# Graph network kernel: the table fill issued by SP during the counting phase, and all row fetches in the fused rank-and-sum phase

## The chip, the cores and the metric

The kernel runs on one core of a Trainium2 chip. A core has five engines with queues of their own: TensorE (PE: matmuls, and PEld for its weight loads), VectorE (DVE), ScalarE (ACT), GpSimd (POOL) and SyncE (SP), and 16 DMA engines that all of them share. The metric is the device time of one execution in microseconds (us), lower is better.

## The reference, cut to what matters

Four graph layers run one after another over 50,000 nodes of 128 features and 25,000 edges, each followed by a layer norm. The change touches only the first, and of it the part ahead of the matmul:

```python
loops = jnp.arange(N); src = concat([edge_index[0], loops]); dst = concat([edge_index[1], loops])
deg = segment_sum(ones, dst);  dinv = rsqrt(deg)
msg = (x @ W)[src] * (dinv[src] * dinv[dst])[:, None]
h = segment_sum(msg, dst) + b            # then batch norm, relu, x + h
...
x = layernorm(x + L0(x, ...))            # then L1 (routing), L2 (attention), L3 (mean)
```

The kernel sums the rows x[src] times dinv[src] for every dst into a table `agg` in HBM (50,000 x 128, zero where no edge ends), and does the rest from there.

## The kernel before, in words

The program is a row of phases. Each is a Block in which every engine has its own list of instructions; a Block ends when all five engines are through their lists, and a short Block of GpSimd that clears the semaphores follows. Nothing of the next phase starts before that. Edges lie as 200 columns of 128 (T = 200), handled in 50 groups of four columns (EG = 50, GT = 4). The phases that the change touches:

- `ids_phase` (L83): SP loads the src and dst ids with six DMAs (L106 to L109), DVE and PE turn them into columns, SP stores them as rows (L113, L114). ACT issues in this phase, through `fill` (L77), the 49 DMAs that write zeros to all of `agg`, 512 KB each (L80, called at L119).
- `order_phase` (L557): SP loads the dst row once more, shifted by one (L584), PE turns it, and DVE works out which edge is the last of its dst.
- `count_phase` (L207): DVE builds one-hot tiles from the ids in 16 bits (`lows` L254, `highs` L262) and PE adds them up into two histograms (L304); a short chain on DVE, ACT and PE at the end makes the degrees and start positions (L269 to L284). GpSimd fetches the rows x[src] of the first EARLY = 24 groups, one indirect DMA of 128 rows for each column (L242), into the tile `x_src`, which has room for all 200 columns. SP waits for the fill (L233).
- `rank_and_sum_phase` (L325), the fused phase: per column DVE makes one-hot tiles (L428, L431, 16 bit) and compares (L438, L452, L455), PE looks up rank and dinv (L519, L525, L533, L534), ACT weighs the row that was fetched (L504), PE sums edges of one dst (L544, L549), ACT copies the sum to a buffer (L496; US = 3 buffers of a group each). GpSimd fetches the rows of the other 26 groups (L389) and scatters every group's sums to `agg` (L398), four indirect DMAs for each group.
- `moments_phase` reads `agg` and follows.

The order on each queue is written out by `pipeline` (L1549): in step m it calls each stage, in the order given, for the group m minus its lag. For GpSimd it is `pipeline(EG, (late_gather, 0), (scatter, 1))` (L408), where `late_gather` fetches a group in the first two steps and then in every second. A fetch waits only for the fetch four groups before (SC = 4). `scatter(g)` waits until ACT has copied group g; ACT's copy of group g waits for the scatter of group g - 3; ACT's weighing of a column waits for the fetch of its group (L502).

Of the kernel before, what the change touches and what calls it, by code (L numbers as in the profile page):

```python
# [28 lines left out]
SC = 4  # L29
# [3 lines left out]
GT = 4  # L33
EG = T // GT
NJ = 8
NG = N // (P * NJ)
# [46 lines left out]
def ids_phase(k):  # L83

    nc = k.nc
    with ExitStack() as st:
        rows = k.sb(st, "ids_rows_i", [TB, 2, 2, P], I32)
        rows_f = k.sb(st, "ids_rows_f", [TB, 2, 2, P])
        low = k.sb(st, "ids_low_i", [TB, 2, 2, P], I32)
        low_f = k.sb(st, "ids_low_f", [TB, 2, 2, P])  # L90
        cols_i = k.sb(st, "ids_cols_i", [P, 2, T], I32)
        part = k.sb(st, "ids_part_i", [P, 2, 2, T], I32)
        minus = k.sb(st, "ids_minus", [1, 1])
        pt = k.ps(st, "ids_pt", [P, 2, 2, 256])
        padded = k.sem(st, "ids_padded")
        loaded = k.sem(st, "ids_loaded")
        step = k.sem(st, "ids_step")
        turned = k.sem(st, "ids_turned")
        stored = k.sem(st, "ids_stored")
        with nc.Block() as block:  # L100
            @block.sync
            def _(sp):
                sp.wait_ge(padded, 1)
                full = (E // P - TB)
                for a, ids in enumerate((k.src, k.dst)):
                    sp.dma_start(rows[:, a, 0, :], ids[0:TB * P].rearrange("(r e) -> r e", e=P)).then_inc(loaded, 16)  # L106
                    sp.dma_start(rows[0:full, a, 1, :],
                                 ids[TB * P:(TB + full) * P].rearrange("(r e) -> r e", e=P)).then_inc(loaded, 16)
                    sp.dma_start(rows[full:full + 1, a, 1, 0:E - (TB + full) * P],  # L109
                                 ids[(TB + full) * P:E].rearrange("(r e) -> r e", r=1)).then_inc(loaded, 16)  # L110
                sp.wait_ge(step, 3)
                for a, row in enumerate((k.src_row, k.dst_row)):
                    sp.dma_start(row[0:EP].rearrange("(b r e) -> r b e", b=2, e=P), rows_f[:, a]).then_inc(stored, 16)  # L113
                sp.dma_start(k.dst_row[EP:EP + 1].rearrange("(r e) -> r e", r=1), minus[:, :]).then_inc(stored, 16)  # L114
                sp.wait_ge(stored, 48)

            @block.scalar
            def _(act):
                fill(k, act, k.agg, k.zeros[:, :].rearrange("p (j d) -> p j d", j=NJ), k.agg_filled)  # L119

            @block.vector
            def _(dve):
                nc.vector.memset(minus[:, :], -1.0)
                nc.vector.memset(rows[:, :, :, :], PAD_ID).then_inc(padded, 1)
                dve.wait_ge(loaded, 96)
                nc.vector.tensor_copy(rows_f[:, :, :, :], rows[:, :, :, :]).then_inc(step, 1)
                nc.vector.tensor_scalar(low[:, :, :, :], rows[:, :, :, :], 3, 127, ALU.arith_shift_right,
                                        ALU.bitwise_and).then_inc(step, 1)
                dve.wait_ge(step, 2)
                nc.vector.tensor_copy(low_f[:, :, :, :], low[:, :, :, :]).then_inc(step, 1)  # L130

                dve.wait_ge(turned, 1)
                nc.vector.tensor_copy(k.id_col[:, 0, :, :], pt[:, :, 0, 0:T]).then_inc(step, 1)
                nc.vector.tensor_copy(cols_i[:, :, :], pt[:, :, 0, 0:T]).then_inc(step, 1)
                nc.vector.tensor_copy(k.low_col16[:, :, :], pt[:, :, 1, 0:T]).then_inc(step, 1)
                dve.wait_ge(step, 5)
                nc.vector.tensor_scalar(part[:, 0, :, :], cols_i[:, :, :], 10, 3, ALU.arith_shift_right,
                                        ALU.arith_shift_left).then_inc(step, 1)
                nc.vector.tensor_scalar(part[:, 1, :, :], cols_i[:, :, :], 7, None, ALU.bitwise_and).then_inc(step, 1)
                nc.vector.tensor_scalar(k.node_idx[:, :, :], k.id_col[:, 0, :, :], float(N - 1), None, ALU.min)  # L140
                dve.wait_ge(step, 8)
                nc.vector.tensor_tensor(k.high_col[:, :, :], part[:, 0, :, :], part[:, 1, :, :],
                                        ALU.add).then_inc(step, 1)
                dve.wait_ge(step, 9)

            @block.tensor
            def _(pe):
                pe.wait_ge(step, 3)
                for a in range(2):
                    for b in range(2):  # L150
                        nc.tensor.transpose(pt[:, a, 0, b * TB:(b + 1) * TB], rows_f[:, a, b, :], k.ident[0:TB, 0:TB])
                        last = nc.tensor.transpose(pt[:, a, 1, b * TB:(b + 1) * TB], low_f[:, a, b, :],
                                                   k.ident[0:TB, 0:TB])
                last.then_inc(turned, 1)
        k.done = [padded, loaded, step, turned, stored]
        clear_semaphores(nc, k.done)
# [44 lines left out]
        clear_semaphores(nc, [made, step])  # L201


EARLY = 24


def count_phase(k, rows):  # L207


    nc = k.nc  # L210
    with ExitStack() as st:
# [10 lines left out]
        used = k.sem(st, "cnt_used")  # L222
        step = k.sem(st, "cnt_step")
        based = k.sem(st, "cnt_based")
        in0 = list(k.gather_base)
        for u in range(SC):
            k.gather_base[u] += EARLY // SC * 16 * GT
        rooted = k.sem(st, "cnt_rooted")
        with nc.Block() as block:  # L229
            @block.sync  # L230
            def _(sp):

                sp.wait_ge(k.agg_filled, 16 * (NG + 1))  # L233

            @block.gpsimd
            def _(pool):
                for g in range(EARLY + SC):
                    if g >= SC:
                        pool.wait_ge(k.gathered[g % SC], in0[g % SC] + g // SC * 16 * GT)
                    if g < EARLY:  # L240
                        for t in range(g * GT, (g + 1) * GT):
                            nc.gpsimd.indirect_dma_start(  # L242
                                out=rows[:, t, :], out_offset=None, in_=k.x,
                                in_offset=bass.IndirectOffsetOnAxis(ap=k.node_idx[:, 0, t:t + 1], axis=0))\
                                .then_inc(k.gathered[g % SC], 16)

            @block.vector
            def _(dve):
# [44 lines left out]
            def _(pe):  # L293
# [4 lines left out]
                for n in range(T):  # L298
# [4 lines left out]
                    for a in range(2):  # L303
# [4 lines left out]
                pe.wait_ge(step, 4)  # L308
                nc.tensor.matmul(base[:, 0:1], k.before[:, :], scan[:, NCOL - 1:NCOL], start=True,
                                 stop=True).then_inc(based, 1)  # L310
        clear_semaphores(nc, [low_made, hot, used, step, based, rooted, k.agg_filled])


def paced(eng, k, sem, value):
# [10 lines left out]
def rank_and_sum_phase(k, order, rows):  # L325

    nc = k.nc
    with ExitStack() as st:
# [20 lines left out]
                 "ranked", "weighed", "masked", "summed", "copied"]  # L349
        s = {x: k.sem(st, "rank_" + x) for x in names}  # L350
        in0, out0 = list(k.gather_base), list(k.scatter_base)
        for g in range(EARLY, EG):
            k.gather_base[g % SC] += 16 * GT
        for g in range(EG):
            k.scatter_base[g % US] += 16 * GT

        def landed(g):
            return in0[g % SC] + (g - EARLY) // SC * 16 * GT + 16 * GT

        def stored(g):  # L360
            return out0[g % US] + g // US * 16 * GT + 16 * GT
# [1 line left out]
        with nc.Block() as block:  # L363
# [18 lines left out]
            def _(pool):  # L382
                nc.gpsimd.iota(eid[:, :], pattern=[[P, T]], base=0, channel_multiplier=1).then_inc(s["numbered"], 1)

                def gather(g):
                    if g >= EARLY + SC:
                        pool.wait_ge(k.gathered[g % SC], landed(g - SC))
                    for t in range(g * GT, (g + 1) * GT):
                        nc.gpsimd.indirect_dma_start(  # L389
                            out=rows[:, t, :], out_offset=None, in_=k.x,  # L390
                            in_offset=bass.IndirectOffsetOnAxis(ap=k.node_idx[:, 0, t:t + 1], axis=0))\
                            .then_inc(k.gathered[g % SC], 16)
# [7 lines left out]
                            in_=sums[:, g % US, j, :], in_offset=None, bounds_check=N - 1, oob_is_err=False)\  # L400
                            .then_inc(k.scattered[g % US], 16)

                def late_gather(m):
                    g = EARLY + m if m < 2 else EARLY + 1 + m // 2
                    if (m < 2 or m % 2 == 0) and g < EG:
                        gather(g)

                pipeline(EG, (late_gather, 0), (scatter, 1))  # L408
                for g in range(EG - US, EG):
                    pool.wait_ge(k.scattered[g % US], stored(g))  # L410

# [64 lines left out]
            def _(act):  # L476
# [21 lines left out]

                def weigh(n):
                    g = n // GT  # L500
                    if g >= EARLY:
                        act.wait_ge(k.gathered[g % SC], landed(g))  # L502
                    act.wait_ge(s["dinv_picked"], n + 1)
                    nc.scalar.activation(rows[:, n, :], rows[:, n, :], ACT.Copy, scale=k.dinv_src[:, n:n + 1])\  # L504
                        .then_inc(s["weighed"], 1)
# [2414 lines left out]
def build(nc, a, out):  # L2920
# [3 lines left out]
    with ExitStack() as st:  # L2924
        k.paces = k.sem(st, "paces")

        k.agg_filled = k.sem(st, "agg_filled")
        k.gather_base, k.scatter_base = [0] * SC, [0] * (RF + 2)
        k.gathered = [k.sem(st, f"gathered{u}") for u in range(SC)]
        k.scattered = [k.sem(st, f"scattered{u}") for u in range(RF + 2)]  # L2930
# [53 lines left out]
        with ExitStack() as filling:  # L2984
            x_src = k.sb(filling, "x_src", [P, T, D])
            order_phase(k, by_dst, "ord_d")
            count_phase(k, x_src)
            rank_and_sum_phase(k, by_dst, x_src)
        moments_phase(k)
        capsules_phase(k)  # L2990
# [51 lines left out]
```

## Time and profile before

| what | us |
| --- | --- |
| median of 3 runs | 6120.39 (6107.27 to 6133.74) |
| the profiled execution | 6107.41 |
| its span in the trace | 6105.6 |

| stretch of the span, us | phase |
| --- | --- |
| 4.96 to 67.38 | ids phase, with the fill on ACT's queue |
| 68.37 to 80.38 | order phase |
| 81.23 to 336 | count phase with 96 fetches |
| 344.33 to 778 | fused phase with 104 fetches and 200 scatters |
| from 785.34 | moments and all later phases |

Of the later phases two are named: the message phase (3602 to 4156 us) and the mean phase (4970 to 5517), in which GpSimd fetches and scatters all 200 columns (`segment_sum_phase`, L642, L707 and L719), four and four for each group. Times in a row are from the start of the span. In a timeline row the columns are start, duration, engine, line, operation, output and inputs, count, and in brackets the idle time of the engine just before and what ended it. "issue" there means that the engine waited for nothing that the profile shows.

### The profile page before, as it was taken

To read this page: it belongs to the slowest core of one execution; us is meant where nothing else is said; L and a number is where in the kernel's file an instruction comes from. 1 tells how busy PE (TensorE), PEld (TensorE's weight loads), DVE (VectorE), ACT (ScalarE), POOL (GpSimd) and SP (SyncE) were. 2 spreads that over 40 slices of the span, in tenths; PEclk is the share of its full clock that TensorE was granted. 3 is DMA by queue.
4 is the path that set the end of the run, shared out by engine and by line. 5 is a ranking of instruction groups with operands and counts; after the bars stand their busy time and mean duration, and the time that the engine had idled before them with its cause. 6 is when DMAs were issued, how large, how long until landed. Compare 5 with 4: busy or idle time off the path is not lost. (4 is left out here: it accounts for less than half of the span.)

```text
span 6105.6 us, 71185 instructions
## 1 busy us (share of the span) xinstructions
PE 3580.9 (59%) x20428; PEld 2837.0 (46%) x20428; DVE 3790.8 (62%) x11171; ACT 2487.7 (41%) x5939; POOL 2997.5 (49%) x2581
## 2 busy tenths in 40 slices
PE   3379955874111366630667337666999956664443
PEld 0046644773000255530666225554777745554442
DVE  5579944996222466522777656664766635556998
ACT  0046554994000255520222114443666631124666
POOL 4867702730777433376777127772111137772221
PEclk9789977997555689855888655667999977776666
DMA  4023387883444577621555647773434436665554
GB/s 178 24 82 107 99 322 254 254 253 121 130 147 151 189 254 251 204 83 43 154 155 155 214 105 264 262 260 119 147 140 138 142 102 210 211 217 175 188 187 147
DMA packets 555804, 1043.94 MB, mean 171 GB/s; under 512 B 102981, under 2 KB 320489, under 8 KB 549102
## 3 DMA queue, kind: packets, MB, share of 16 engines
q1 hardware_dynamic: 447424, 830.52, 41.0%
q0 software_dynamic: 92800, 157.14, 8.9%
q10 hardware_dynamic: 15192, 51.73, 2.2%
q8 instruction: 167, 2.74, 0.2%
q14 instruction: 221, 1.81, 0.1%
HBM read 663.92 MB, written 387.58 MB: 172 GB/s over the span
## 5 line engine op out<-in xcount | busy, mean ns | idle before, releaser
L1911 PE MATMUL ro_end<-vals,end_mask 128*2 128x128 f32 x1600 | 243.9, 318 | 569.2 <-DVE vals L1775 472.1
L2078 POOL DMA_INDIRECT sc_rows<-layer,node_idx x400 | 388.3, 971 | 155.9 <-issue 121.5
L1911 PEld LDWEIGHTS ro_end<-vals,end_mask 128*2 128x2 f32 x1600 | 148.4, 96 | 655.4 <-DVE vals L1775 483.7
L2524 POOL TENSOR_TENSOR tf_rest<-tf_rest,tf_msum 128x1024 f32<-128x1024 f32 (+1 forms) x49 | 128.8, 2628 | 627.8 <-DMA tf_rest<-rest 627.8
L2587 ACT ACTIVATE tf_hidden<-tf_h_ps,tf_b 128x512 f32<-128x512 f32 x392 | 268.8, 687 | 233.0 <-PE tf_h_ps L2626 222.5
L2638 PE MATMUL tf_o_ps<-tf_w,tf_hidden 128*128 128x128 f32 (+1 forms) x3136 | 358.0, 275 | 0.0
L1937 PE MATMUL ro_acc<-vals,ro_mask 128*126 128x128 f32 x1600 | 246.3, 319 | 187.6 <-ACT ro_square L1869 140.7
L1713 POOL DMA_INDIRECT ro_far<-layer,w_far x200 | 214.7, 1074 | 287.7 <-DVE ro_y L1752 227.1
L2638 PEld LDWEIGHTS tf_o_ps<-tf_w,tf_hidden 128*128 128x128 f32 (+1 forms) x3136 | 353.9, 192 | 0.5 <-issue 0.5
L1235 POOL DMA_INDIRECT sorted<-payload,rank x200 | 198.2, 991 | 316.3 <-POOLq L70 252.0
L2626 PE MATMUL tf_h_ps<-tf_x_t,tf_w 128*128 128x512 f32 x784 | 349.9, 599 | 5.1 <-ACT tf_hidden L2587 3.9
L707 POOL DMA_INDIRECT msg_rows<-values,s_eid x200 | 211.1, 1055 | 272.4 <-POOLq L70 211.8
L937 PE MATMUL ml_conv_out<-op_w_t,ml_conv_tsb 128*128 128x128 f32 (+1 forms) x784 | 177.2, 418 | 281.3 <-DVEq L2864 277.7
L2840 POOL TENSOR_TENSOR ml_scaled<-ml_scaled,op_gamma 128x1024 f32<-128x1024 f32 (+1 forms) x49 | 116.2, 2371 | 450.0 <-ACT ml_scaled L1020 450.0
L1937 PEld LDWEIGHTS ro_acc<-vals,ro_mask 128*126 128x126 f32 x1600 | 227.6, 228 | 210.4 <-issue 175.2
L1726 POOL TENSOR_TENSOR vals<-ro_both,ro_weight 126x1024 f32<-126x1024 f32 x75 | 144.9, 1933 | 336.3 <-ACT ro_weight L1893 333.9
L937 PEld LDWEIGHTS ml_conv_out<-op_w_t,ml_conv_tsb 128*128 128x128 f32 (+1 forms) x784 | 165.3, 320 | 293.9 <-ACT ml_conv_tsb L923 286.4
L242 POOL DMA_INDIRECT x_src<-in_x_dram,node_idx x96 | 222.7, 2320 | 109.4 <-SPq L229 80.5
L1759 DVE TENSOR_TENSOR ro_both<-ro_far,ro_y 128x1024 f32<-128x1024 f32 x25 | 31.0, 1238 | 392.1 <-DMA ro_y<-layer,w_own 392.1
L707 POOL DMA_INDIRECT mean_rows<-x,node_idx x200 | 215.0, 1075 | 118.3 <-POOLq L70 57.7
L1739 POOL DMA_INDIRECT layer<-ro_far,w_last x200 | 215.3, 1076 | 96.5 <-issue 60.4
L398 POOL DMA_INDIRECT agg<-rank_sums,d_last x200 | 212.0, 1060 | 74.4 <-issue 60.9
(474 smaller groups left out, 11932.6 us busy)
## 6 DMA issues: line engine op xcount, KB each, us to landing
ro_mask<-masks SPq DMA_DIRECT2D x100, 504.0 KB, 4.9
si_both<-layer SPq DMA_DIRECT2D x48, 1024.0 KB, 6.1
ro_far<-far SPq DMA_DIRECT2D x75, 512.0 KB, 6.1
ro_both<-both SPq DMA_DIRECT2D x75, 512.0 KB, 6.1
agg<-zeros ACTq DMA_DIRECT2D x48, 512.0 KB
mom_x<-in_x_dram SPq DMA_DIRECT2D x48, 512.0 KB, 9.2
mom_agg<-agg SPq DMA_DIRECT2D x48, 512.0 KB, 7.7
y<-mom_y SPq DMA_DIRECT2D x48, 512.0 KB, 8.5
```

The lines of the kernel that those rows point to most:

```text
L242: nc.gpsimd.indirect_dma_start(out=rows[:, t, :], out_offset=None, in_=k.x, in_offset=bass.IndirectOffsetOnAxis(ap=k.node_idx[:, 0, t:t + ...
L398: nc.gpsimd.indirect_dma_start(out=k.agg, out_offset=bass.IndirectOffsetOnAxis(ap=order.last_idx[:, t:t + 1], axis=0), in_=sums[:, g % US, ...
L707: nc.gpsimd.indirect_dma_start(out=rows[:, g % SS, j, :], out_offset=None, in_=table, in_offset=bass.IndirectOffsetOnAxis(ap=index[:, t:t ...
L937: mm = self.k.nc.tensor.matmul(self.out[b][0:p, j, :], self.turned_sb[:, 4 * b + j, 0:p], self.weight, start=plain, stop=plain or j == 3, ...
L1713: nc.gpsimd.indirect_dma_start(out=rows, out_offset=None, in_=k.layer1_halves, in_offset=bass.IndirectOffsetOnAxis(ap=column[real, t:t + 1 ...
L1739: nc.gpsimd.indirect_dma_start(out=k.layer1_halves, out_offset=bass.IndirectOffsetOnAxis(ap=wide.last[real, t:t + 1], axis=0), in_=sent[re ...
L1911: mm = nc.tensor.matmul(end_ps[0:2, j, :], k.end_mask[:, t, :], k.vals[:, t, :], start=True, stop=True, skip_group_check=True)
L1937: mm = nc.tensor.matmul(acc[w][real, j, :], mask[:, u, j, :], k.vals[:, tile(n, j), :], start=True, stop=True, skip_group_check=True)
L2078: nc.gpsimd.indirect_dma_start(out=rows[:, g % SC, c * GT + j, :], out_offset=None, in_=k.layer1, in_offset=bass.IndirectOffsetOnAxis(ap=k ...
L2587: nc.scalar.activation(hidden[:, h, b, :], h_ps[b][:, :], ACT.Relu, bias=b1[:, b:b + 1]).then_inc(s["bent"], 1)
L2626: nc.tensor.matmul(h_ps[b][:, :], w1[:, b * P:(b + 1) * P], x_t[:, u, 4 * h:4 * h + 4, :].rearrange("p j e -> p (j e)"), start=True, stop= ...
L2638: mm = nc.tensor.matmul(o_ps[h][0:p, j, :], hidden[:, h, b, j * P:j * P + p], w2[:, b, :], start=b == 0, stop=b == NB - 1)
```

## The change

ACT's fill in the ids phase goes away; SP issues the same 49 DMAs at the start of the count phase and waits for them there. GpSimd does nothing in the count phase. In the fused phase it fetches all 50 groups, one in each step, and scatters with a lag of three groups and not one.

```diff
@@ ids_phase
-            @block.scalar
-            def _(act):
-                fill(k, act, k.agg, k.zeros[:, :].rearrange("p (j d) -> p j d", j=NJ), k.agg_filled)
@@ count_phase
-        in0 = list(k.gather_base)
-        for u in range(SC):
-            k.gather_base[u] += EARLY // SC * 16 * GT
+        filled = k.sem(st, "cnt_filled")
...
             def _(sp):
-                sp.wait_ge(k.agg_filled, 16 * (NG + 1))
-            @block.gpsimd
-            def _(pool):
-                for g in range(EARLY + SC):
-                    if g >= SC:
-                        pool.wait_ge(k.gathered[g % SC], in0[g % SC] + g // SC * 16 * GT)
-                    if g < EARLY:
-                        for t in range(g * GT, (g + 1) * GT):
-                            nc.gpsimd.indirect_dma_start(
...
+                fill(k, sp, k.agg, k.zeros[:, :].rearrange("p (j d) -> p j d", j=NJ), filled)
+                sp.wait_ge(filled, 16 * (NG + 1))
@@ rank_and_sum_phase
-            return in0[g % SC] + (g - EARLY) // SC * 16 * GT + 16 * GT
+            return in0[g % SC] + g // SC * 16 * GT + 16 * GT
...
-                    if g >= EARLY + SC:
+                    if g >= SC:
                         pool.wait_ge(k.gathered[g % SC], landed(g - SC))
...
-                def late_gather(m):
-                    g = EARLY + m if m < 2 else EARLY + 1 + m // 2
-                    if (m < 2 or m % 2 == 0) and g < EG:
-                        gather(g)
-                pipeline(EG, (late_gather, 0), (scatter, 1))
+                pipeline(EG, (gather, 0), (scatter, 3))
...
-                    if g >= EARLY:
+                    if n % GT == 0:
                         act.wait_ge(k.gathered[g % SC], landed(g))
```

GpSimd's queue before, from the clearing ahead of the count phase (L74) into the fused phase; `x_src` are fetches and `agg` scatters:

```order
L74 ISA x5
L70 UNCONDITIONAL_BRANCH
L235 UNCONDITIONAL_BRANCH
L242 DMA x_src<-in_x_dram,node_idx 128x128 x96
L229 UNCONDITIONAL_BRANCH
L71 UNCONDITIONAL_BRANCH
L74 ISA x7
L70 UNCONDITIONAL_BRANCH
L381 UNCONDITIONAL_BRANCH
L383 IOTA rank_eid 128x200
L389 DMA x_src<-in_x_dram,node_idx 128x128 x8
L398 DMA agg<-rank_sums,d_last 50000x128 x4
```

The same queue of the changed kernel, with the first groups of the fused phase:

```order
L74 ISA x7
L70 UNCONDITIONAL_BRANCH
L361 UNCONDITIONAL_BRANCH
L363 IOTA rank_eid 128x200
L369 DMA x_src<-in_x_dram,node_idx 128x128 x16
L378 DMA agg<-rank_sums,d_last 50000x128 x4
L369 DMA x_src<-in_x_dram,node_idx 128x128 x4
L378 DMA agg<-rank_sums,d_last 50000x128 x4
```

The 96 fetches ahead of the phase are gone, the phase starts with 16 fetches and not with 8, and then fetches and scatters alternate by fours (before: 4 fetches, 8 scatters). SP's queue before, from the end of the ids phase to the fused phase:

```order
L114 DMA dst_row<-ids_minus 1x1
L100 UNCONDITIONAL_BRANCH
L573 UNCONDITIONAL_BRANCH
L584 DMA ord_d_next<-dst_row 100x2x128
L572 UNCONDITIONAL_BRANCH
L230 UNCONDITIONAL_BRANCH
L229 UNCONDITIONAL_BRANCH
L364 UNCONDITIONAL_BRANCH
L369 DMA rank_src_b<-src_row 128x512
```

SP's queue of the changed kernel at the same place:

```order
L114 DMA dst_row<-ids_minus 1x1
L100 UNCONDITIONAL_BRANCH
L548 UNCONDITIONAL_BRANCH
L559 DMA ord_d_next<-dst_row 100x2x128
L547 UNCONDITIONAL_BRANCH
L221 UNCONDITIONAL_BRANCH
L80 DMA agg<-zeros 128x1024 x48
L80 DMA agg<-zeros 106x1024
L220 UNCONDITIONAL_BRANCH
L344 UNCONDITIONAL_BRANCH
L349 DMA rank_src_b<-src_row 128x512
```

The 49 DMAs of the fill now stand behind the ids and the shifted row, and ahead of nothing but the end of the count phase.

## Rows read from the trace of the kernel before

**Rows 1.** Busy time by engine in stretches of the first 480 us.
```profile
core 0: us, PE busy (x) PEld busy (x) DVE busy (x) ACT busy (x) POOL busy (x), PEclk, DMA share, GB/s
0.00:67.00 67.00, 1.60 (x8) 1.29 (x8) 7.63 (x26) 0.00 (x0) 0.92 (x7) 1.00 0.93 368
...
130.00:180.00 50.00, 29.81 (x133) 7.69 (x132) 50.00 (x164) 0.00 (x0) 50.00 (x1) 1.00 0.00 0
...
244.00:344.00 100.00, 0.00 (x0) 0.00 (x0) 0.00 (x0) 0.00 (x0) 67.91 (x72) 0.50 0.17 48
...
380.00:480.00 100.00, 100.00 (x492) 66.27 (x491) 99.13 (x434) 60.29 (x198) 77.64 (x74) 1.00 0.36 98
```
**Rows 2.** Timeline of the ids and order phases.
```profile
4.96 62.42 ACTq L80 DMA_DIRECT2D agg<-zeros  x49
...
5.68 0.42 SPq L106 DMA_DIRECT2D ids_rows_i<-in_src_dram  x1
...
9.63 1.18 SPq L109 DMA_DIRECT2D ids_rows_i<-in_dst_dram  x1
...
15.14 0.43 DVE L126 CAST ids_rows_f<-ids_rows_i 100x512 f32<-100x512 int32 x1 [9.49 <-DMA ids_rows_i<-in_dst_dram]
...
20.34 0.57 DVE L142 TENSOR_TENSOR high_col<-ids_part_i 128x400 f32<-128x400 int32 x1
...
68.37 0.28 SPq L584 DMA_DIRECT2D ord_d_next<-dst_row  x1
...
77.86 0.59 PE L634 MATMUL ord_d_pt<-ident,ord_d_next 100*128 100x100 f32 x2 [59.84 <-DMA ord_d_next<-dst_row]
...
80.11 0.27 DVE L619 CAST d_last<-ord_d_cols 128x200 int32<-128x200 f32 x1
...
81.26 1.29 DVE L254 TENSOR_TENSOR cnt_hot_low<-iota_row,low_col 128x512 f16<-128x512 f16 x2 [0.88 <-PEq L70]
```
**Rows 3.** Timeline of the second order phase, with no fill beside it.
```profile
1487.63 0.28 SPq L584 DMA_DIRECT2D ord_s_next<-sorted_row  x1
...
1489.85 0.60 PE L634 MATMUL ord_s_pt<-ident,ord_s_next 100*128 100x100 f32 x2 [2.87 <-DMA ord_s_next<-sorted_row]
```
**Rows 4.** Timeline of the count phase and of the next start.
```profile
88.74 1.93 DVE L262 TENSOR_SCALAR cnt_hot_high<-iota_high,high_col 128x392 f16<-128x392 f16 x8
...
91.79 1.93 DVE L262 TENSOR_SCALAR cnt_hot_high<-iota_high,high_col 128x392 f16<-128x392 f16 x8
...
92.48 1.81 PE L304 MATMUL cnt_table<-cnt_hot_high,cnt_hot_low 128*128 128x392 f16 x8 [1.25 <-DVE cnt_hot_high L262]
...
124.69 2.75 POOL L242 DMA_INDIRECT x_src<-in_x_dram,node_idx  x1 [0.30 <-issue]
127.75 107.32 POOL L242 DMA_INDIRECT x_src<-in_x_dram,node_idx  x1 [0.31 <-issue]
...
229.27 1.92 DVE L262 TENSOR_SCALAR cnt_hot_high<-iota_high,high_col 128x392 f16<-128x392 f16 x8
...
232.32 1.92 DVE L262 TENSOR_SCALAR cnt_hot_high<-iota_high,high_col 128x392 f16<-128x392 f16 x8
...
235.37 0.94 POOL L242 DMA_INDIRECT x_src<-in_x_dram,node_idx  x1 [0.30 <-issue]
...
332.79 0.94 POOL L242 DMA_INDIRECT x_src<-in_x_dram,node_idx  x1 [0.30 <-issue]
...
242.48 0.43 DVE L284 TENSOR_SCALAR start<-cnt_scan,cnt_base 128x392 f32<-128x392 f32 x1
...
344.36 0.29 POOL L383 IOTA rank_eid<- 128x200 int32 x1 [10.62 <-POOLq L70]
```
**Rows 5.** Groups of instructions on GpSimd in the first 900 us.
```profile
L398 POOL DMA_INDIRECT agg<-rank_sums,d_last x200 | 212.0, 1060 | 74.4 <-issue 60.9 <-ACT rank_sums L496 13.4
...
L389 POOL DMA_INDIRECT x_src<-in_x_dram,node_idx x104 | 112.4, 1080 | 31.8 <-issue 31.8
```
**Rows 6.** Timeline of GpSimd in the fused phase.
```profile
368.64 1.51 POOL L398 DMA_INDIRECT agg<-rank_sums,d_last  x1 [13.14 <-ACT rank_sums L496]
...
488.48 0.99 POOL L389 DMA_INDIRECT x_src<-in_x_dram,node_idx  x1 [0.30 <-issue]
...
504.79 0.99 POOL L389 DMA_INDIRECT x_src<-in_x_dram,node_idx  x1 [0.30 <-issue]
...
753.29 0.98 POOL L398 DMA_INDIRECT agg<-rank_sums,d_last  x1 [0.30 <-issue]
...
774.20 0.98 POOL L398 DMA_INDIRECT agg<-rank_sums,d_last  x1 [0.30 <-issue]
```
**Rows 7.** Busy time of GpSimd's fetches (L707, 200 each) in two later phases.
```profile
4970.00:5517.00 547.00, 215.02 (x200) 0.77 0.63 204
3602.00:4156.00 554.00, 211.08 (x200) 0.61 0.75 252
```
**Rows 8.** Busy time by engine in stretches of the mean phase.
```profile
5050.00:5250.00 200.00, 138.91 (x749) 119.56 (x750) 110.79 (x129) 41.13 (x112) 155.13 (x148) 0.78 0.64 208
...
5205.00:5210.00 5.00, 0.77 (x4) 0.50 (x4) 3.43 (x4) 0.00 (x0) 4.03 (x4) 0.84 0.67 245
5210.00:5215.00 5.00, 5.00 (x20) 4.24 (x20) 2.62 (x4) 1.11 (x4) 3.84 (x4) 0.50 0.16 49
```

More of the change, by code:

```diff
@@ L201, in constants_phase, with count_phase @@
         clear_semaphores(nc, [made, step])
-EARLY = 24
-def count_phase(k, rows):
+def count_phase(k):
     nc = k.nc
@@ L231, in _ @@
             def _(sp):
-                sp.wait_ge(k.agg_filled, 16 * (NG + 1))
-            @block.gpsimd
-            def _(pool):
-                for g in range(EARLY + SC):
-                    if g >= SC:
-                        pool.wait_ge(k.gathered[g % SC], in0[g % SC] + g // SC * 16 * GT)
-                    if g < EARLY:
-                        for t in range(g * GT, (g + 1) * GT):
-                            nc.gpsimd.indirect_dma_start(
-                                out=rows[:, t, :], out_offset=None, in_=k.x,
-                                in_offset=bass.IndirectOffsetOnAxis(ap=k.node_idx[:, 0, t:t + 1], axis=0))\
-                                .then_inc(k.gathered[g % SC], 16)
+                fill(k, sp, k.agg, k.zeros[:, :].rearrange("p (j d) -> p j d", j=NJ), filled)
+                sp.wait_ge(filled, 16 * (NG + 1))
             @block.vector
@@ L310, in _ @@
                                  stop=True).then_inc(based, 1)
-        clear_semaphores(nc, [low_made, hot, used, step, based, rooted, k.agg_filled])
+        clear_semaphores(nc, [low_made, hot, used, step, based, rooted, filled])
 def paced(eng, k, sem, value):
@@ L351, in rank_and_sum_phase @@
         in0, out0 = list(k.gather_base), list(k.scatter_base)
-        for g in range(EARLY, EG):
+        for g in range(EG):
             k.gather_base[g % SC] += 16 * GT
@@ L2925, in build @@
         k.paces = k.sem(st, "paces")
-        k.agg_filled = k.sem(st, "agg_filled")
         k.gather_base, k.scatter_base = [0] * SC, [0] * (RF + 2)
@@ L2986, in build @@
             order_phase(k, by_dst, "ord_d")
-            count_phase(k, x_src)
+            count_phase(k)
             rank_and_sum_phase(k, by_dst, x_src)
```

## The prediction, made before the changed kernel had run

> **What bounds the kernel now.** I read the stretches of busy time first, to see which phases have an engine that is never idle, and then the timeline of each phase that the change touches.
>
> The count phase is in two halves [rows 1]. From 130 to 180 DVE is busy all of the time and so is GpSimd, but GpSimd with one instruction. From 244 to 344 nothing works but GpSimd. The timeline says why [rows 4]: while DVE makes its 16-bit one-hots, a fetch takes 2.75 us and then one takes 107.32 us; as soon as DVE is through, at 235, it takes 0.94 us plus 0.30 of issue. So only 17 of the 96 fetches were given out beside the counting, and the other 79 run from 235.37 to 333.73 with no cover. DVE's chain had ended at 242.91, and the fused phase begins at 344.36.
>
> The ids and order phases wait for the fill [rows 1, 2]: the DMA engines are 93% busy with it, ACT is busy issuing it until 67.38 though the ids were ready at 20.91, and the shifted row, issued at 68.37, lands only before 77.86 because it stands behind the rest of the fill.
>
> The fused phase is bound twice over. PE and DVE are busy for 100% and 99% of 380 to 480 [rows 1]. GpSimd shows 77.6% there, which looks like room, but every indirect DMA has 0.30 us of "issue" before it, and from the first scatter on the two group rows hold no other idle time to speak of (60.9 and 31.8 us of "issue" in 198 and 104 gaps, 13.4 of waiting, nearly all of it the one wait before the first scatter) [rows 5, 6]. A block of 4 fetches and 8 scatters takes 504.79 - 488.48 = 16.31 us and serves two groups, just what DVE and PE need: 8.15 us a group. In the mean phase, where GpSimd issues 8 indirect DMAs a group, it is busy for 155.13 us of 200, 78% as well [rows 8]. That share is therefore GpSimd's full speed.
>
> **Part 1, the fill leaves the ids phase.** The order phase and the count phase start earlier. Counting from before's own rows [rows 2]: the six loads start at 5.68; the last is issued at 9.63 and the data are there at 15.14. Without 25 MB in the queues I take the issue at 8 and the landing 3 us later, 11. The landing is an estimate between the 2.2 us of the small load with free queues [rows 3] and the 5.5 us here. DVE's and PE's chain from there takes 20.91 - 15.14 = 5.8, to 16.8, with SP's stores beside it. The end of the Block takes 68.37 - 67.38 = 1.0. The shifted row takes 2.2 and not 9.5 [rows 3]. From there to the first one-hot 81.26 - 77.86 = 3.4. Counting starts at 23.4 and not at 81.26: **-58 us**. Bounds: if the ids land no sooner than before, -53; if all small transfers are faster by another 2 us, -60.
>
> **Part 2, the fill in the count phase.** SP has nothing else there. 49 issues took 62.4 us and the rest drained in some 10 more, so it is over at about 96 and DVE's counting, 161.65 us long, at 185. I cost it at nothing; the cover is 89 us thick. Nothing is queued behind SP's wait but the end of the phase. The loads of the fused phase come after it, as they came after SP's wait before. No row shows DVE counting beside such a transfer; a slowing by 1% of the 73 us that it lasts would be under 1 us.
>
> **Part 3, no fetches in the count phase.** The phase ends after DVE's chain, 161.65 us from its start. The Block end costs 81.26 - 80.38 = 0.9 where GpSimd has issued no DMA [rows 2]; behind 96 fetches it cost 10.6 [rows 4]. The fused phase starts 0.9 us behind DVE's chain and not 344.36 - 242.91 = 101.4: **-100 us**. Upper bound of the time: with the 10.6 kept, -91. DVE's speed does not change: a group of four columns took 91.79 - 88.74 = 3.05 us beside the fetches and 232.32 - 229.27 = 3.05 when GpSimd gave out nothing [rows 4].
>
> **Part 4, 96 more fetches on GpSimd's queue in the fused phase.** This is a cost, since that queue has no free time. Before, from its start at 344.36 to the end of the last scatter at 775.18 it is 430.8 us. Now: 16 fetches at 1.25 plus 0.7, 20.7 us. The first scatter waits until ACT has copied group 0, as before 24.3 us behind the start, so 13 us of idle time shrink to 3.5. Then 384 indirect DMAs without a gap.
>
> Their price, with the 0.30 in it: before, 296 of them took 775.18 - 368.64 = 406.5, that is 1.373 each. Undisturbed ones take 0.98 + 0.30 (scatter) and 0.94 + 0.30 (fetch) [rows 4, 6], 376 us for the 296; so 30 us are delays. If the delays stay as many as DVE's 16-bit instructions, the 384 cost 486 + 30 = 516. If they grow with the number of DMAs, 525. In the mean phase 400 of them took 547 in all, 1.367 with waits [rows 7]. I take 1.35 x 384 = 518. With 24.3 ahead it is 542.7: **+112 us**. Bounds: no delays at all, 486, +80; the price of the slower later phase, 554 / 400 = 1.385 [rows 7], +125.
>
> Whether a group now waits on something else: DVE and PE need 8.15 us a group and GpSimd gives one every 10.8, so they wait for the fetch (ACT's wait ahead of weighing) some 2.6 us each group. The scatter of group g stands behind the fetch of g + 3, when group g was copied long ago, so GpSimd waits for nobody. The tail stays: the last scatter, then 10 us to the moments phase.
>
> The Trainium skill (SBUF — State Buffer, section "Who interferes with whom") says that a DVE instruction in a two-port mode and GpSimd lock each other out for a whole instruction, first come first served. By that rule the delays follow the number of DVE's instructions, which is the 516 above and not the 525; both lie within 5 us of what I took.
>
> **Sum.** -58 - 100 + 112 = -46. On the profiled execution 6107.4 - 46 = 6061.4; on the median, which is 13 us above it, 6120.4 - 46 = **6074.4 us**, a ratio of 0.9925. Unknowns at their ends: -60 - 101 + 80 = -81, 6039; -53 - 91 + 125 = -19, 6101.
>
> **Rivals.**
>
> *PE's clock falls a little in the new pauses.* Now PE never rests in the fused phase and the granted clock is 1.00. In the mean phase a stretch in which PE did 0.77 us of work in 5 is followed by one at 0.50, that is 1.2 GHz, though PE is then busy throughout [rows 8]; over that phase it is 0.77, and 0.61 over the other [rows 7]. For it: the new pauses of 2.6 us come once a group. Against it: in counting PE pauses 1.25 us in every 3.05 and keeps 1.00 [rows 1, 4]; and the effect checks itself, since a slower PE fills its own pause. Price: at the mean phase's 0.77 a group takes PE 8.15 / 0.77 = 10.6 us, still inside GpSimd's 10.8. At 0.73 it is 11.2, 50 x (11.2 - 8.15) = 152 on the phase: -6 in all, 6114. No difference, chance 0.10.
>
> *The clock falls for good, and the kernel is slower.* The same mechanism in force: at the message phase's 0.61 [rows 7] a group takes 8.15 / 0.61 = 13.4 us, 50 x 5.25 = 262 us on the phase: +104, 6224. It decides from 8.15 + 158 / 50 = 11.3 us a group on, a mean clock of 0.72. Chance 0.06. The Trainium skill (TensorE: Matmul & The Clock Gate, section "HAM oscillation") warns of this: a kernel that waits for a transfer in each round restarts cold in each round. The row of 5210 agrees that it happens; no row shows it for pauses of 2.6 us after 8 us of unbroken work.
>
> *GpSimd's indirect DMAs get cheaper.* With DVE idle a quarter of the time, its locks fall into gaps: the lower bound of part 4, +80, 6042. Chance 0.08.
>
> *The moved work is not hidden at all or not moved.* The queue listings show it moved, so I give it nothing.
>
> **How the numbers follow.** Forecast with its bounds 0.76, of which 0.07 lie at the upper edge within 0.5%. A measurement of this kernel can tell about 0.5% (31 us) from no change. Faster by more: 0.69 + 0.08 = 0.77. Within: 0.07 + 0.10 = 0.17. Slower: 0.06. The range takes the bounds 6039 and 6101 with a few us of scatter between runs: 6040 to 6104. It leaves out the two clock cases and slips at the edges, 0.2.
>
> **What the changed profile would show.** Part 1: first one-hot of counting at 22 to 28. Part 3: the fused phase begins 162.5 us behind it, near 186. Part 2: the fill's DMAs on SP's queue from there, landed before 105, and DVE's groups still 3.05 us. Part 4: GpSimd without gaps above 0.3 us from the first scatter, 10.6 to 11 us from group to group, PE busy 75 to 80%, and ACT's largest wait the one for `x_src`. Wrong it would be if DVE is still at 99% there (then GpSimd had room), if the granted clock in the fused phase is below 0.9, or if the last scatter comes earlier than 515 or later than 560 us behind the start.

## The result, and the profile after

| | before | changed |
| --- | --- | --- |
| median, us | 6121.7 (4 runs, 6107.3 to 6133.7) | 6071.7 (4 runs, 6060.0 to 6076.7) |
| span of the profiled execution, us | 6105.6 | 6074.9 |
| ratio | | 0.9917, 95% interval 0.9889 to 0.9944 |

The changed kernel is 50 us faster by the medians. The forecast was 6074.4 with a range of 6040 to 6104.

The ids and order phases of the changed kernel, timeline (the answer to [rows 2]):

```profile
7.48 0.28 SPq L109 DMA_DIRECT2D ids_rows_i<-in_dst_dram  x1
9.32 0.43 DVE L122 CAST ids_rows_f<-ids_rows_i 100x512 f32<-100x512 int32 x1 [3.67 <-DMA ids_rows_i<-in_dst_dram]
...
14.51 0.56 DVE L138 TENSOR_TENSOR high_col<-ids_part_i 128x400 f32<-128x400 int32 x1
...
16.12 0.28 SPq L559 DMA_DIRECT2D ord_d_next<-dst_row  x1
...
18.18 0.59 PE L609 MATMUL ord_d_pt<-ident,ord_d_next 100*128 100x100 f32 x2 [5.99 <-DMA ord_d_next<-dst_row]
...
21.58 1.29 DVE L234 TENSOR_TENSOR cnt_hot_low<-iota_row,low_col 128x512 f16<-128x512 f16 x2 [0.88 <-PEq L70]
```

The ids land at 9.3 and not at 15.1, the shifted row 2.1 us after its issue and not 9.5, and counting starts at 21.58 and not at 81.26. The largest piece lies between the two: the ids are ready at 15.07 and the order phase begins 1.05 us later, where before it began 47.46 us after the ids were ready (20.91 to 68.37), since the Block could not end while ACT was still issuing. Of the 59.7 us, 46.4 are this wait for ACT's issuing, 5.8 the landing of the ids and 7.4 the shifted row. The busy times by stretch (the answer to [rows 1]):

```profile
core 0: us, PE busy (x) PEld busy (x) DVE busy (x) ACT busy (x) POOL busy (x), PEclk, DMA share, GB/s
0.00:20.00 20.00, 2.19 (x10) 1.58 (x10) 8.77 (x31) 0.00 (x0) 0.92 (x7) 1.00 0.09 25
20.00:80.00 60.00, 36.91 (x156) 10.58 (x156) 59.05 (x194) 1.28 (x1) 0.00 (x0) 1.00 0.98 389
80.00:180.00 100.00, 56.60 (x252) 14.82 (x250) 99.75 (x316) 0.53 (x1) 0.00 (x0) 0.99 0.06 23
...
400.00:500.00 100.00, 84.60 (x369) 54.29 (x370) 74.42 (x319) 44.97 (x151) 76.81 (x77) 0.93 0.35 91
```

From 20 to 80 the DMA engines are 98% busy with the fill, and DVE counts beside them; the fill is over long before the counting. The row of before in which only GpSimd worked has gone. In the fused phase, in the stretch from 400 to 500, DVE has fallen from 99% to 74%, PE from 100% to 85%, and GpSimd stands at 77%, as before. Its rows (the answer to [rows 4] and [rows 6]):

```profile
182.66 0.43 DVE L264 TENSOR_SCALAR start<-cnt_scan,cnt_base 128x392 f32<-128x392 f32 x1
184.27 0.29 POOL L363 IOTA rank_eid<- 128x200 int32 x1 [182.71 <-POOLq L70]
```

```profile
440.76 0.99 POOL L369 DMA_INDIRECT x_src<-in_x_dram,node_idx  x1 [0.31 <-issue]
...
451.12 1.00 POOL L369 DMA_INDIRECT x_src<-in_x_dram,node_idx  x1 [0.30 <-issue]
...
462.16 0.99 POOL L369 DMA_INDIRECT x_src<-in_x_dram,node_idx  x1 [0.31 <-issue]
...
721.45 0.98 POOL L378 DMA_INDIRECT agg<-rank_sums,d_last  x1 [0.30 <-issue]
```

One group takes 10.4 and 11.0 us, and the gaps are 0.3 us of issue. The groups of GpSimd, and who waited for whom in the phase (engine, line, waited for: us in total, times, longest):

```profile
L378 POOL DMA_INDIRECT agg<-rank_sums,d_last x200 | 207.3, 1037 | 63.4 <-issue 60.4 <-ACT rank_sums L471 3.0
L369 POOL DMA_INDIRECT x_src<-in_x_dram,node_idx x200 | 205.9, 1029 | 61.2 <-issue 60.3 <-ACT rank_sums L471 0.9
```

```profile
ACT rank_low_hot L463 <- PE rank_turned L494: 117.1, 148, 2.5
DVE rank_picked L427 <- PE rank_look L509: 99.3, 68, 5.9
ACT rank_sums L471 <- DMA agg<-rank_sums,d_last: 82.5, 30, 5.1
...
ACT x_src L479 <- DMA x_src<-in_x_dram,node_idx: 47.8, 26, 4.2
```

GpSimd waited for work once, 2.74 us ahead of the first scatter at 208.87; the rest of the 3.0 and 0.9 us put down to ACT are gaps of 0.30 us like all others. ACT waits for GpSimd through its scatters and its fetches. Its longest wait in total, the 117.1 us for PE, is no sign of that: it was there before (114.4).

All kernels of this study run the same instructions from the moments phase on. This table takes the main points of each profiled execution apart, from their timelines and groups (us; "chain" is from the first one-hot to the start of the last instruction of DVE's chain, "fused" from the start of the phase to the start of the last scatter, "rest" from the first load of the moments phase to the end of the span):

| kernel | counting starts | chain | fused starts | fused | moments start | rest |
| --- | --- | --- | --- | --- | --- | --- |
| before | 81.3 | 161.2 | 344.4 | 429.8 | 785.3 | 5320.3 |
| changed | 21.6 | 161.1 | 184.3 | 537.2 | 729.7 | 5345.3 |
| e1_fill_only | 21.9 | 161.2 | 287.6 | 429.7 | 728.4 | 5327.2 |
| e2_fetch_only | 80.9 | 161.1 | 243.6 | 538.0 | 789.8 | 5341.4 |
| e3_early_4_groups | 21.8 | 161.2 | 185.0 | 516.0 | 708.9 | 5329.9 |
| e4_early_12_groups | 21.9 | 161.3 | 226.3 | 477.0 | 715.4 | 5338.0 |
| e5_lag_2 | 21.9 | 161.1 | 184.6 | 541.6 | 734.1 | 5334.8 |
| e7_two_input_onehots | 22.5 | 283.9 | 308.0 | 476.9 | 797.0 | 5341.5 |
| e8_paced_dve | 22.1 | 162.4 | 195.9 | 476.1 | 684.2 | 5340.6 |
| e9_paced_tighter | 26.3 | 163.6 | 191.6 | 476.7 | 680.4 | 5331.1 |
| e10_early_24_paced | 26.7 | 163.1 | 247.6 | 430.7 | 689.4 | 5328.8 |
| e11_early_24_one_wait | 26.4 | 161.3 | 274.9 | 431.0 | 717.0 | 5343.3 |

The rest varies by 25 us from one execution to the next, with no order in it. That is the scatter of this measurement, and the reason why the two profiled spans differ by 31 us and the medians by 50. Where two kernels have the same instructions in the first 730 us, the pieces agree within about 1 us (537.2 and 538.0; 477.0, 476.9, 476.1 and 476.7), so these can be compared closely, the whole only by the median of several runs.

### The profile page after: what moved, and what is told of

Read it like the earlier page. It is cut to its first block and busy times, and to the rows that moved or that the text cites. A ratio compares the mean times of both kernels' runs of the same rounds, so it can differ in the third digit from the quotient of the medians.

```text
span 6074.9 us, 71017 instructions
## 1 busy us (share of the span) xinstructions
PE 3601.1 (59%) x20317; PEld 2864.6 (47%) x20428; DVE 3792.9 (62%) x11171; ACT 2480.6 (41%) x5939; POOL 2876.7 (47%) x2581
## 3 DMA queue, kind: packets, MB, share of 16 engines
q8 instruction: 167, 2.74, 0.2%
## 5 line engine op out<-in xcount | busy, mean ns | idle before, releaser
L1714 POOL DMA_INDIRECT layer<-ro_far,w_last x200 | 221.0, 1105 | 96.1 <-issue 60.3
L694 POOL DMA_INDIRECT msum<-msg_sent,s_last x200 | 206.4, 1032 | 77.6 <-issue 59.2
L694 POOL DMA_INDIRECT agg<-mean_sums,d_last x200 | 210.8, 1054 | 62.9 <-issue 60.3
```

Of the source, the lines that this page charges most:

```text
L694: nc.gpsimd.indirect_dma_start(out=dest, out_offset=bass.IndirectOffsetOnAxis(ap=order.last_idx[:, t:t + 1], axis=0), in_=sent[:, g % SS, ...
L1714: nc.gpsimd.indirect_dma_start(out=k.layer1_halves, out_offset=bass.IndirectOffsetOnAxis(ap=wide.last[real, t:t + 1], axis=0), in_=sent[re ...
```

## The experiments

**Which part brings the gain.** Two kernels, each with one part of the change. The first:

```diff
 # before.py, count_phase; ACT's fill in the ids phase removed
             def _(sp):
+                fill(k, sp, k.agg, k.zeros[:, :].rearrange("p (j d) -> p j d", j=NJ), k.agg_filled)
                 sp.wait_ge(k.agg_filled, 16 * (NG + 1))
```

> The kernel before with the fill alone moved: SP issues it at the start of the count phase; the 96 fetches beside the counting stay. Theory (fill is the whole net gain, the move of the fetches is neutral: 100 us saved in the count phase, 107 added in the fused phase, 3 back at its end): counting starts near 21.6 us in the span and not at 81.3, the fused phase starts near 284.7, and all of -60 us stays: ratio to before 0.990 (6062 against 6122), within 0.3% of the changed kernel. Rival (the fill's move alone gives little since GpSimd's fetches bound the count phase and the fill slows them): -20 us or less, ratio 0.997 or more.

Measured: 6057.5 us, ratio 0.9899 (0.9884 to 0.9913). The second, the fetches alone:

```diff
 # changed kernel, ids_phase
+            @block.scalar
+            def _(act):
+                fill(k, act, k.agg, k.zeros[:, :].rearrange("p (j d) -> p j d", j=NJ), k.agg_filled)
 # count_phase
-                fill(k, sp, k.agg, k.zeros[:, :].rearrange("p (j d) -> p j d", j=NJ), filled)
-                sp.wait_ge(filled, 16 * (NG + 1))
+                sp.wait_ge(k.agg_filled, 16 * (NG + 1))
...
```

> The changed kernel with the fill put back on ACT's queue in the ids phase; all 200 fetches in the fused phase. Theory: count phase 100 us shorter, fused phase 107 us longer, end of it 3 us shorter, so ratio to before 1.000 to 1.001 (+4 us). Rival (moving the fetches is where the gain is, as the 100 us without other work in the count phase suggest): -40 us, ratio 0.993.

Measured: 6125.1 us, ratio 1.0006 (0.9995 to 1.0017). The table shows the pieces: fetches in the fused phase start it 100.4 us earlier behind the counting (162.7 and not 263.1 us after the first one-hot), make it 108 us longer, and save 3 us at its end (7.2 and not 10.2 us from the end of the last scatter to the moments phase). The whole gain of the change is the fill's 60 us. The first kernel, without the move, is even a little faster by its median (6057.5 against 6071.7), though the intervals of the two ratios overlap; up to the moments phase they lie 1.3 us apart. Moving the fetches has no effect that the medians can tell from none (up to the moments phase it costs 4.5 us), since GpSimd's time was only carried from a place where it stood alone to one where it stands alone again.

**Is it GpSimd's stream that bounds the fused phase?** If so, each indirect DMA taken out of the phase is worth 1.34 us there. Sixteen of them go beside the counting:

```diff
 # changed kernel, count_phase
+            @block.gpsimd
+            def _(pool):
+                for g in range(EARLY):                    # EARLY = 4
+                    for t in range(g * GT, (g + 1) * GT):
+                        nc.gpsimd.indirect_dma_start(out=rows[:, t, :], ...)
...
 # rank_and_sum_phase, fetches spread evenly between the scatters
-                pipeline(EG, (gather, 0), (scatter, 3))
+                fetched = EARLY
+                for g in range(EG):
+                    while fetched < min(EG, EARLY + 4 + -(-g * (EG - EARLY - 4) // (EG - 4))):
+                        gather(fetched)
+                        fetched += 1
+                    scatter(g)
```

> The changed kernel with the first 4 groups (16 fetches) issued beside the counting, without a wait between them; the other 184 spread evenly over the fused phase. Theory (GpSimd's instruction stream is the bound of the fused phase at 1.34 us for each indirect DMA): 16 x 1.34 = 21 us less in the fused phase, 517 and not 538, the count phase as long as in the changed kernel, so ratio to before 0.988 (6050). Rival (ACT's waits for scatters, 82 us in the changed kernel, bound it rather than the number of DMAs): the fused phase stays at 535 or more.

Measured: 6041.3 us, ratio 0.9878 (0.9859 to 0.9896). The phase took 516.0 us where 517 was expected. With 12 groups out early it took 477.0 where 474 was expected (e4, below). That is 1.2 to 1.3 us for each DMA taken out. With 24 groups it took 430.7 (e10, below), the floor, where PE and DVE are at 100 and 99% again.

The other candidate was the wait of ACT for a buffer, of which the prediction had said nothing:

```diff
-                pipeline(EG, (gather, 0), (scatter, 3))
+                pipeline(EG, (gather, 0), (scatter, 2))
```

> The changed kernel with the scatters two groups and not three behind the fetches. In the changed kernel ACT waits 82.5 us for a buffer that a scatter still holds, and 47.8 for fetched rows; the prediction had named only the latter. Theory (GpSimd's stream of 400 indirect DMAs at 1.34 us is the bound, the waits of the others are its shadow): the phase stays at 537 +- 4 us, ACT's wait only shifts from scatters to fetches, ratio to the changed kernel 1.000 +- 0.002. Rival (the wait for buffers costs time by itself): the phase falls by 10 us or more.

Measured: 6070.7 us, ratio to before 0.9912 (0.9897 to 0.9927), the changed kernel 0.9917. The fused phase took 541.6 us, 4.5 more, just past the expected 537 +- 4.

```profile
ACT x_src L479 <- DMA x_src<-in_x_dram,node_idx: 122.1, 47, 3.8
```

ACT's wait for scatters is gone from the longest waits and the one for fetches has grown from 47.8 to 122.1, with nothing gained. These waits are the shadow of one queue; which of them is seen depends on the order in it. The 4.5 us are GpSimd's own, and all lie in one place: only 12 fetches and not 16 stand ahead of the first scatter now, so it waits there 7.19 us for ACT's first copy and not 2.74. After that every gap is 0.30 us again.

**Why were the fetches beside the counting held?** In [rows 4] the 17th fetch takes 107 us. It is also the first with a semaphore wait ahead of it. Twelve groups without any wait between them:

> As the one with 4 groups, but 12 groups (48 fetches) beside the counting, with no semaphore wait between the groups (before had one ahead of the 17th fetch, the one that took 107 us). Theory A (the wait ahead of the fifth group is what held GpSimd until DVE ended): all 48 go at 3.05 us each, over by 170 us, hidden; the fused phase falls to 24 + 336 x 1.34 = 474; ratio to before 0.981 (6007). Theory B (whatever the waits, GpSimd gets no more than some 16 fetches out while DVE makes 16-bit one-hots): the 17th again takes over 100 us, the other 31 follow at 1.25 behind DVE's end, the fused phase starts 40 us later; ratio 0.988 (6048).

Measured: 6055.3 us, ratio 0.9892 (0.9878 to 0.9906). Theory B, and with less than 16. Timeline of GpSimd with 4 groups early, where there are only 16 fetches and no wait:

```profile
56.06 2.75 POOL L237 DMA_INDIRECT x_src<-in_x_dram,node_idx  x1 [0.30 <-issue]
59.12 116.49 POOL L237 DMA_INDIRECT x_src<-in_x_dram,node_idx  x1 [0.30 <-issue]
175.91 0.94 POOL L237 DMA_INDIRECT x_src<-in_x_dram,node_idx  x1 [0.30 <-issue]
```

It was the 14th here, the 13th with 12 groups, the 15th in e1 and the 17th in before. Neither the semaphore nor a count of 16 decides it: the fetch is let go when DVE's counting ends. Where the slow ones end is seen in the fourth fetch of before, beside DVE's row of 88.74 to 90.67 in [rows 4]:

```profile
88.04 2.75 POOL L242 DMA_INDIRECT x_src<-in_x_dram,node_idx  x1 [0.30 <-issue]
```

It ends 0.1 us behind the last of the eight TENSOR_SCALARs, and so do the others of 2.75 us. The long ones end 0.7 to 0.8 us behind the last TENSOR_SCALAR ahead of the end of DVE's counting (234.25 and 235.07 in before). This points at the TENSOR_SCALARs, the only instructions with one 16-bit input in DVE's loop. The next kernel is the one with 12 groups with another form of them:

```diff
-                        nc.vector.tensor_scalar(hot_high[:, n % 4, a, :], k.iota_high16[:, :],
-                                                k.high_col[:, a, n:n + 1], None, ALU.is_equal).then_inc(hot, 1)
+                        nc.vector.scalar_tensor_tensor(hot_high[:, n % 4, a, :], k.iota_high16[:, :],
+                                                       k.high_col[:, a, n:n + 1], ones16[:, :], ALU.is_equal,
+                                                       ALU.mult).then_inc(hot, 1)
```

> The one with 12 groups beside the counting, with the one-hots of the high ids made by an instruction with two inputs from SBUF (compare, then times a tile of ones) and not with one: same output, other form on DVE, which costs DVE more, up to 96 us in all. Theory (it is DVE's 16-bit one-input form that shuts GpSimd out): no fetch takes more than 3 us, most near 1, and all 48 are out within 70 us of the start of counting. Rival (any DVE work without gaps does it): again one fetch of over 100 us.

Measured: 6140.3 us, a single run and so without an interval; the instruction takes 622 ns and not 304, so counting took 284 us, more than I had allowed for. And the theory fell, as did its rival:

```profile
52.39 5.20 POOL L238 DMA_INDIRECT x_src<-in_x_dram,node_idx  x1 [0.31 <-issue]
57.89 5.20 POOL L238 DMA_INDIRECT x_src<-in_x_dram,node_idx  x1 [0.30 <-issue]
```

Here too the fetches go one to a group from the fifth on: 5.20 us and 0.30 make 5.50, which is DVE's time for one group of four columns there, as 3.05 is in the others. But none was held longer than that. So the two-input form slows fetches as well; what only the one-input form did here is to hold one fetch over many groups. With one run this is seen, not proven to be the form's doing: the instructions are also twice as long.

**Can a pause of DVE let a held fetch in?** Again with 12 groups and the old form of DVE's instructions. GpSimd counts a semaphore up behind each fetch, and DVE asks for it:

```diff
+                        pool.sem_inc(sent, 1)          # behind each fetch
...
                 for g in range(EG):
+                    if 0 <= g - 2 < EARLY * GT:
+                        dve.wait_ge(sent, g - 2 + 1)
                     lows(g)
```

> The one with 12 groups beside the counting; GpSimd counts a semaphore up behind each fetch, and DVE waits ahead of group g of the counting until fetch g - 2 is out. Theory (a fetch that has missed its place is held only as long as DVE goes on without a pause; a short pause lets it in): no fetch over 7 us, 48 of them out by 180 us, counting at most 15 us longer, fused phase 477 as with 12 groups unpaced, ratio to before 0.984 (6024). Rival (GpSimd then falls behind for good and DVE pays 1 us and more in every group): counting 50 us longer or more, ratio 0.989 or more.

Measured: 6021.3 us, ratio 0.9836 (0.9819 to 0.9852). GpSimd and DVE of this kernel at the place:

```profile
62.44 46.23 POOL L238 DMA_INDIRECT x_src<-in_x_dram,node_idx  x1 [0.30 <-issue]
108.98 1.28 POOL L238 DMA_INDIRECT x_src<-in_x_dram,node_idx  x1 [0.30 <-issue]
```

```profile
105.91 1.94 DVE L261 TENSOR_SCALAR cnt_hot_high<-iota_high,high_col 128x392 f16<-128x392 f16 x8
108.75 1.29 DVE L253 TENSOR_TENSOR cnt_hot_low<-iota_row,low_col 128x512 f16<-128x512 f16 x2 [0.90 <-POOLq L242]
```

The 15th fetch was held for 46 us and came free in the one pause of DVE, of 0.90 us, 15 groups later, again 0.8 us behind DVE's last TENSOR_SCALAR. "No fetch over 7 us" was wrong: the semaphore is counted by GpSimd's queue ahead of its work, so the waits up to a count of 26 were met with 14 fetches done, and only the one for 27 stopped DVE. The part of the theory that a pause of under 1 us is enough was borne out, by this one pause. Asking earlier:

```diff
-                    if 0 <= g - 2 < EARLY * GT:
-                        dve.wait_ge(sent, g - 2 + 1)
+                    if g + 8 <= EARLY * GT:
+                        dve.wait_ge(sent, g + 8)
```

> The paced kernel with 12 groups beside the counting, with DVE waiting ahead of group g for the semaphore to reach g + 8 and not g - 1. In the paced kernel the semaphore ran ahead of the work: the 15th fetch was held for 46 us, and DVE stopped for 0.9 us only when group 28 asked for a count of 27, so GpSimd's queue had counted 11 more than it had done. Theory (a held fetch is let in by a pause of under 1 us, whenever it comes): each held fetch now lasts about 12 to 18 us and not 46, all 48 are out near 180, the fused phase starts at 187 and not at 196, ratio to before 0.9825 (6013). Rival (each pause is followed by another holding soon, or DVE waits in every group): counting over 10 us longer, no gain over the paced kernel.

Measured: 6016.0 us, ratio 0.9820 (0.9807 to 0.9834), the fastest kernel of this study. The expected number came, but not for the expected reason:

```profile
22.56 1.16 POOL L238 DMA_INDIRECT x_src<-in_x_dram,node_idx  x1 [21.00 <-POOLq L70]
...
26.28 1.29 DVE L253 TENSOR_TENSOR cnt_hot_low<-iota_row,low_col 128x512 f16<-128x512 f16 x2 [5.38 <-POOLq L242]
...
40.22 2.14 DVE L261 TENSOR_SCALAR cnt_hot_high<-iota_high,high_col 128x392 f16<-128x392 f16 x8
40.82 0.94 POOL L238 DMA_INDIRECT x_src<-in_x_dram,node_idx  x1 [0.30 <-issue]
...
61.17 0.94 POOL L238 DMA_INDIRECT x_src<-in_x_dram,node_idx  x1 [0.30 <-issue]
61.38 1.28 DVE L253 TENSOR_TENSOR cnt_hot_low<-iota_row,low_col 128x512 f16<-128x512 f16 x2
```

No fetch was held at all. DVE waited once, at the start; from then on all fetches took some 0.94 us beside DVE at work, the longest 1.25, the last began at 83.1, and DVE's chain grew by only 2.4 us. The fetch at 40.82 lies wholly within eight TENSOR_SCALARs, which took 2.14 us and not 1.93. GpSimd and DVE can run side by side at nearly full speed, then. I took the head start of the first fetch for the reason and tried 24 groups with the same waits, and with the one wait at the start alone (`if g == 0: dve.wait_ge(sent, 8)`):

> The tighter paced kernel with 24 groups (96 fetches) beside the counting and not 12, as many as in the kernel before. With 12, none was held: the first fetch had started 3.7 us ahead of DVE's first one-hot, not 0.7 us behind it as in all kernels before it, and all 48 went at 1.25 us beside DVE, which took 3.1 us a group and not 3.05. Theory (a GpSimd stream that is under way when DVE starts keeps its pace): 96 fetches over by 22.6 + 96 x 1.25 = 143 us, counting 163 to 167 us long, fused phase again 430 us as before (DVE and PE bound, 304 indirect DMAs), so 47 us less than with 12 groups: ratio to before 0.9745 (5972). Rival (it holds only for a while; from some point on fetches are held again): fused phase starts 30 to 60 us later, ratio 0.980 or more.

> The same 24 groups with a single wait of DVE, ahead of the first group of the counting, for a count of 8, and none after it. Theory (who starts first decides, the later waits never bind): same as with all waits, ratio 0.9745. Rival (the later waits do the work, as DVE yields at each): fetches of 2.75 us and then one over 50 us appear again, ratio 0.985 or more.

Measured: 6033.3 us, ratio 0.9859 (0.9836 to 0.9881), and 6048.2, ratio 0.9870 (0.9840 to 0.9899). Both rivals. The head start was the same, 3.7 us, but after ten and eight fetches the profile shows the old pace again, 2.75 us each, and later a long one. In the first kernel it took 37.05 us and was let go by a pause of DVE of 0.89:

```profile
82.79 37.05 POOL L238 DMA_INDIRECT x_src<-in_x_dram,node_idx  x1 [0.30 <-issue]
119.91 1.29 DVE L253 TENSOR_TENSOR cnt_hot_low<-iota_row,low_col 128x512 f16<-128x512 f16 x2 [0.89 <-POOLq L242]
120.15 1.27 POOL L238 DMA_INDIRECT x_src<-in_x_dram,node_idx  x1 [0.30 <-issue]
```

In the second, which had no pauses, there were two:

```profile
91.22 8.86 POOL L238 DMA_INDIRECT x_src<-in_x_dram,node_idx  x1 [0.30 <-issue]
100.39 79.83 POOL L238 DMA_INDIRECT x_src<-in_x_dram,node_idx  x1 [0.30 <-issue]
```

The first of them, over three groups, ended without any pause of DVE; the second ended with DVE's counting. So a head start is not enough, and since e9 and e10 are alike up to the fetch where they part, neither is it the number of fetches. The pace changes within one execution. Whether it also changes from one execution to the next is not shown: each kernel was profiled once, and the runs of the second spread from 6010 to 6062 us, those of before beside them from 6092 to 6133. Nor is it excluded that the chip matters, since e9 ran on another one than e10 and e11. What the condition is stays open. Shown is that there are three paces (1.25 us, one a DVE group, none for many groups), that a pause of DVE of under 1 us ended the third in both kernels in which one fell into it (e8, e10), and that the fused phase of the 24-group kernel is 430.7 us. By an estimate from these rows (476.7 - 430.7), a kernel which kept the first pace for 96 fetches would save another 46 us.

## Why the prediction was right

Point by point, by its own steps:

- *Fill out of the ids phase, -58:* measured 21.6 - 81.3 = -59.7. The landing of the ids was the estimate in it (11; measured 9.3).
- *Fill beside the counting, at nothing:* DVE's chain took 161.1 and not 161.2 us with the DMA engines at 98% for the first 60.
- *No fetches in the count phase, -100:* the fused phase starts 162.7 us behind the first one-hot and not 263.1, -100.4.
- *96 more fetches in the fused phase, +112:* measured 537.2 - 429.8 = +107.4. The price of the 384 indirect DMAs was 513.6 us, 1.337 each, and not 518. The value that goes by the number of DVE's instructions, 516, was nearer than the one that goes by the number of DMAs, 525; the Trainium skill's rule (SBUF — State Buffer, section "Who interferes with whom") stood behind the former. More kernels say the same: 336 indirect DMAs took 453.3 us in e4, so 48 more took 60.3, or 1.26 each, about the undisturbed price. The delays did not grow with the number of DMAs.
- *End of the phase, taken as equal:* 2.9 us shorter. Not foreseen, and not explained here; over all kernels it takes from 6.9 to 11.2 us.
- *Sum:* -55.6 us at the start of the moments phase, where -46 was forecast: 10 us off, from small errors that all went one way. The medians moved by 50, and the rest of the program scatters by 25. That the measured median lies only 3 us from the forecast is therefore luck; that it lies in the range is not.

Its other signs were right (GpSimd without gaps, about 10.7 us a group, DVE far below 99%) but for three. Counting was to start at 22 to 28 and started at 21.58. It named the fetch as ACT's largest wait; of ACT's waits for GpSimd the one for the scatter was larger, and the one for PE larger still. In "GpSimd waits for nobody" it had looked at what GpSimd waits for and not at ACT's copy of group g, which needs the scatter of g - 3, which now stands behind the fetch of g. e5 shows that this costs nothing. And PE was busy 84 to 85%, above the 75 to 80 given.

The clock rivals were weighed with 0.16 together, and the clock did fall, in a form without price: in stretches of 100 us from 200 to 700 the granted clock was between 0.93 and 0.98, where it had been 1.00 from 380 to 680 before. PE was busy for 84 to 85% and the phase went on at GpSimd's pace, in line with the argument that a slower PE fills its own pauses.

The main step that made the number good was to read 77.6% of busy as full. Every gap was 0.30 us and named "issue", so the queue had no room, and 100 us in which the other engines stood idle could not be had for nothing.

## What to carry to other kernels

An engine whose gaps are all the smallest gap may be full, whatever its busy share says; here work moved to it cost its whole price, and work that moved from one place where it bounds the time to another gained nothing. Look for what blocks a short phase first: 25 MB of zeros that nobody needed before 368 us cost 60 us, 46 of them since the Block could not end before they were issued, and only 13 by slowing some small transfers. When two engines disturb each other in one phase, try a smaller overlap and a short pause of the faster one before giving the overlap up: 48 fetches beside the counting with a paced DVE gave a kernel that gains twice what the change does (0.982 against 0.992), though part of that was an overlap that the pacing is not shown to have caused.

## What the hardware showed that I had not expected

- An indirect DMA of GpSimd can be held for as long as DVE works without a pause: 107, 113, 116 and 119 us in four kernels, from the 13th to 17th fetch on, and 80 us in e11 from the 29th. A pause of 0.90 and of 0.89 us ended it at 46 and 37 us in two others.
- The fetches of 2.75 us beside DVE end 0.1 us behind its eight 16-bit TENSOR_SCALARs, the long ones 0.7 to 0.8 us behind the last of them.
- An instruction of DVE with two inputs from SBUF slowed GpSimd's fetches too (5.20 us each, one run), where I had expected it not to.
- The same fetches beside the same DVE work can also run at 1.25 us each and cost DVE 2.4 us in 161 (e9). The pace can change within one execution (e10, e11); what sets it is open.
- A semaphore that GpSimd counts up behind an indirect DMA is counted before the DMA instruction is done: it had reached 26 with 14 of them done (e8).
